# A hand-written order of 303 work steps, replaced by another order of the same steps

## The reference

```python
x = x + mixer_a(layernorm(x))       # projection to 5 k columns, causal conv over 4 taps, SiLU,
                                    # then attention with decay and Fenwick-level weights, 32 heads
x = x + ffn(layernorm(x))           # 16-head softmax attention, layernorm, 8 experts
                                    # (128 -> 256 -> 128) of which each token uses its best two
x = x + mixer_b(layernorm(x))       # value times 9 gates at 9 shifts along the sequence, layernorm
x = x + ffn(layernorm(x))           # the same ffn, same weights, a second time
```

## Time and profile before

| | us |
|---|---|
| median of 3 runs (2266.46 to 2270.33) | 2267.56 |
| the profiled execution | 2270.33 |
| its span, first to last instruction | 2268.5 |
| PE busy in the span | 2076.0 (92%) |
| DVE busy | 1775.4 (78%) |
| ACT busy | 1447.9 (64%) |
| POOL busy | 874.6 (39%) |

### The profile page before, as it was taken

One profiled execution on the slowest core, in us unless ns is written; L12 is line 12 of the kernel. 1 busy time (PEld: TensorE's weight loads), 2 busy tenths in 40 slices (PEclk: granted clock), 3 DMA queues, 4 the chain that ended last, 5 costly groups with the idle time before them and its releaser, 6 DMA issues. The chain is left out here.

```text
span 2268.5 us, 47559 instructions
## 1 busy us (share of the span) xinstructions
PE 2076.0 (92%) x16832; PEld 1620.4 (71%) x16832; DVE 1775.4 (78%) x4431; ACT 1447.9 (64%) x3113; POOL 874.6 (39%) x1204
## 2 busy tenths in 40 slices
PE   4879899999999999999999999999999999997766
...
PEclk9989999999999999999999999999999999998877
...
DMA packets 185820, 88.01 MB, mean 39 GB/s; under 512 B 118297, under 2 KB 179873, under 8 KB 180417
## 3 DMA queue, kind: packets, MB, share of 16 engines
...
...
## 5 line engine op out<-in xcount | busy, mean ns | idle before, releaser
L1261 DVE TENSOR_REDUCE nmax<-psB 128x2 f32<-128x512 f32 x512 | 315.6, 679 | 34.5 <-PE psB L741 34.4
L1186 DVE SCALAR_TENSOR_TENSOR work<-psA,c_conv_w,work 128x255 f32<-128x255 f32 (+2 forms) x810 | 330.0, 473 | 12.4 <-ACT work L926 12.2
L609 PE MATMUL psA<-xnT_a,c_w_in 128*128 128x256 f32 x1088 | 295.2, 399 | 31.8 <-DVE work L1186 22.7
L1009 ACT ACTIVATE pt<-psB 128x512 f32<-128x512 f32 x512 | 264.5, 609 | 46.1 <-PE psB L760 45.4
L845 PE MATMUL psB<-c_w,hid 128*128 128x128 f32 x2048 | 276.9, 281 | 2.6 <-DVE ff L1342 0.9
L845 PEld LDWEIGHTS psB<-c_w,hid 128*128 128x128 f32 x2048 | 259.9, 194 | 25.0 <-issue 10.1
L833 PE MATMUL psB<-x1T,c_w 128*128 128x256 f32 x1024 | 267.0, 391 | 0.9 <-DVE ff L1342 0.6
L1213 DVE TENSOR_TENSOR att<-att,QK 128x1024 f32<-128x1024 f32 x192 | 238.4, 1270 | 36.0 <-ACT att L963 34.2
L1494 POOL TENSOR_TENSOR own<-X,ccoef 128x512 f32<-128x512 f32 x128 | 160.9, 1266 | 258.5 <-PE psA L674 211.8
L1032 ACT ACTIVATE hid<-psB,c_b 128x256 f32<-128x256 f32 x496 | 211.2, 486 | 75.6 <-PE psB L833 72.3
L963 ACT ACTIVATE att<-psA 128x512 f32<-128x512 f32 x384 | 203.6, 611 | 69.7 <-PE psA L650 67.5
...
## 6 DMA issues: line engine op xcount, KB each, us to landing
qk_scr<-qparts SPq DMA_DIRECT2D x128, 192.0 KB, 3.6
...
low<-lvl_scr SPq DMA_DIRECT2D x256, 1.5 KB
...
```

The source lines that it names most:

```text
L609: e.matmul(t[:, 0:T], w_in[:, first + j * P:first + (j + 1) * P], xnT_a[:, :], start=True, stop=True).then_inc(filled[b], 1)
L1009: e.activation(pt_b[a % PTS][:, :, :].rearrange("p h q -> p (h q)"), t[:, :], ACT.Exp, scale=float(AD) ** -0.5).then_inc(drained[b], 1)
L1186: m = e.scalar_tensor_tensor(out=cv[:, back:], in0=t[:, 0:T - back], scalar=conv_w[:, c, tap:tap + 1], in1=cv[:, back:], op0=ALU.mult, op1 ...
L1261: e.tensor_reduce(nmax[:, i, 2 * h2:2 * h2 + 2], t[:, :].rearrange("p (h k) -> p h k", k=T), AX.X, ALU.max).then_inc(drained[b], 1)
```

## The change

The table `PERIOD` is replaced by another order of the same 303 hops. 292 hops keep their lag. Eleven have one less: `rowmax1.1`, `rowmax1.2`, `rowmax1.3`, `maxt1.0`, `v1.0`, `es1.0`, `exps1.0`, `outp0.2`, `gates0.6`, `place0.0` and `conv0.0`, and ten of them move from the head of a turn to the end of the turn before it, so that they come at nearly the same point of a sequence's life. `place0.0` moves from the middle of a turn to the end of the turn before it, 0.6 of a turn earlier for its sequence. The largest lag stays 5, the turns 21, the table loads of ACT 66. No instruction is added or taken away. L395 goes, and the wait of L603 is put on `conv0.0` and `zgate0.0` of sequence 0.

```diff
 PERIOD = """
-rowmax1.2+4 conv0.0+1 rowmax1.1+4 gates0.6+1 rowmax1.3+4 maxt1.0+4 outp0.2+2 v1.0+4 up0.0+3 fn0.0+2 relu0.0+3
...
+load_x0.0+0 tail0.5+3 up0.0+3 ep1.0+4 fn0.0+2 relu0.0+3 ocopy1.0+4 es1.1+4 lvl0.0+1 exps1.1+4 down1.6+5 fn0.1+2
...
-        first_w_in = next(hop for hop in hops if hop[0] in ("conv", "zgate"))
...
                 elif what in ("conv", "zgate"):
                     first = DIM + conv_tiles(k)[0] * P if what == "conv" else 2 * k * P
-                    if hop == first_w_in:
+                    if n == 0 and k == 0:
                         e.wait_ge(in_loaded, 16 * len(in_consts))
```

More of the change, by code:

```diff
@@ L109 @@
[L109 to L123, removed]
@@ L124 @@
-ep0.1+2 es0.2+2 prod0.3+1 sum0.1+1 ep0.2+2 q1.1+3 sum0.2+1 es0.3+2 sum0.3+1 gated0.1+1 ep0.3+2 exps0.3+2 gates0.3+0
-own0.4+1 gated0.0+1 gated0.2+1 ocopy0.3+2 gated0.3+1 weigh0.4+1 wexp0.4+1 gates0.4+0 wexp0.5+1 up1.5+4 prod0.4+1
-weigh0.5+1 tail0.0+2 sum0.4+1 relu1.5+4 relu1.6+4 own0.5+1 prod0.5+1 gated0.4+1 up1.6+4 wexp0.6+1 tail0.1+2 wexp0.7+1
-gates0.5+0 down1.5+4 weigh0.6+1 acc1.5+4 sum0.5+1 prod0.6+1 relu1.7+4 gated0.5+1 up1.7+4 own0.6+1 tail0.2+2 weigh0.7+1
-sum0.6+1 smax1.0+3 tail0.3+2 prod0.7+1 sum0.7+1 own0.7+1 tail0.4+2 smax1.2+3 outp0.0+1 smax1.1+3 ssq0.0+1 rowmax1.0+3
@@ L129 @@
-ssq0.1+1 ssq0.2+1 ssq0.3+1 smax1.3+3 gated0.6+1 outp0.1+1 gated0.7+1
+load_x0.0+0 tail0.5+3 up0.0+3 ep1.0+4 fn0.0+2 relu0.0+3 ocopy1.0+4 es1.1+4 lvl0.0+1 exps1.1+4 down1.6+5 fn0.1+2
+conv0.1+1 tail0.6+3 q0.0+2 experts0.0+3 ep1.1+4 acc1.6+5 tap0.0+1 ocopy1.1+4 experts0.1+3 es1.2+4 lvl0.1+1
+exps1.2+4 down1.7+5 q0.1+2 up0.1+3 conv0.2+1 taps0.0+1 acc1.7+5 ep1.2+4 down0.0+3 tap0.1+1 es1.3+4 relu0.1+3
+down0.1+3 tap0.2+1 taps0.1+1 acc0.0+3 up0.2+3 up0.3+3 ocopy1.2+4 acc0.1+3 exps1.3+4 relu0.2+3 down0.2+3
@@ new lines @@
+silu0.0+1 experts1.2+5 relu0.3+3 taps0.2+1 zgate0.0+1 acc0.2+3 up0.4+3 down0.3+3 zact0.0+1 conv0.3+1 up0.5+3
+relu0.4+3 tap0.3+1 down0.4+3 silu0.1+1 lvl0.2+1 xt0.0+1 silu0.2+1 conv0.4+1 gates0.0+0 relu0.5+3 acc0.3+3
+experts1.3+5 up0.6+3 up0.7+3 xt0.1+1 taps0.3+1 conv0.5+1 tap0.4+1 silu0.3+1 xcopy0.0+1 acc0.4+3 relu0.6+3
+down0.5+3 tap0.5+1 taps0.4+1 down0.6+3 xcopy0.1+1 relu0.7+3 zgate0.1+1 down0.7+3 xt0.2+1 taps0.5+1 zact0.1+1
+acc0.5+3 acc0.6+3 acc0.7+3 conv0.6+1 tap0.6+1 ep1.3+4 silu0.4+1 ocopy1.3+4 xcopy0.2+1 silu0.5+1 xt0.3+1
@@ new lines @@
+experts0.2+3 taps0.6+1 tail1.0+4 experts0.3+3 conv0.7+1 zgate0.2+1 tap0.7+1 bcp0.0+1 taps0.7+1 xcopy0.3+1
+zact0.2+1 tail1.1+4 mix1.0+3 v0.0+2 xt0.4+1 silu0.6+1 tail1.2+4 xcopy0.4+1 zgate0.3+1 tail1.3+4 silu0.7+1
+smax0.0+2 xt0.5+1 xt0.6+1 mix1.1+3 rowmax0.0+2 zact0.3+1 xcopy0.5+1 smax0.1+2 conv0.8+1 tap0.8+1 tail1.4+4
+smax0.2+2 lvl0.3+1 lvl0.4+1 lvl0.5+1 rowmax0.1+2 lvl0.6+1 xcopy0.6+1 rowmax0.2+2 mix1.2+3 mix1.3+3 tail1.5+4
+tail1.6+4 mix1.4+3 mix1.5+3 taps0.8+1 qk0.0+1 up1.0+4 up1.1+4 relu1.0+4 relu1.1+4 mix1.6+3 experts1.0+4 mix1.7+3
@@ new lines @@
+mix1.8+3 qkc0.0+1 coef0.0+1 experts1.1+4 zgate0.4+1 mix1.9+3 zact0.4+1 mix1.10+3 own0.0+1 down1.0+4 silu0.8+1
+zgate0.5+1 smax0.3+2 zgate0.6+1 zact0.5+1 acc1.0+4 rowmax0.3+2 mix1.11+3 zgate0.7+1 zact0.6+1 lvl0.7+1 up1.2+4
+relu1.2+4 zact0.7+1 maxt0.0+2 mix1.12+3 down1.1+4 acc1.1+4 up1.3+4 weigh0.0+1 weigh0.1+1 wexp0.0+1 down1.2+4
+weigh0.2+1 es0.0+2 prod0.0+1 relu1.3+4 sum0.0+1 wexp0.1+1 exps0.0+2 acc1.2+4 fn1.0+3 wexp0.2+1 down1.3+4
+own0.1+1 fn1.1+3 ep0.0+2 ocopy0.0+2 q1.0+3 gates0.1+0 prod0.1+1 xt0.7+1 es0.1+2 weigh0.3+1 own0.2+1 xcopy0.7+1
```

13 lines of the change are left out of this document (9 added, 4 removed).

## The result

The changed kernel takes 2329.9 us (median of 4 runs, 2328.3 to 2337.3) against 2267.6 for the kernel before (median of 3; a fourth execution of it, in the chip's slower state, took 2444.2 and is left out): the ratio is 1.027, 95% interval 1.025 to 1.030. It is 62 us slower; 31 were forecast (2299, against 2268). The direction was right, the size was half. The time lies inside the whole range given (2240 to 2340) and outside the forecast's own (2284 to 2318). The profiled execution has a span of 2333.7 us.

The account below looks back on a forecast made before the run. PE was taken as the bound, with waits for PSUM banks that DVE frees. New waits of 5.7 against 3.75 us, with 0.2 more, gave 2.2 a turn, 29 in 13 turns, plus 3 in filling: 2299 us, range 2240 to 2340.

Parts of the forecast that it names:

- filling: Turns 1 to 3, as the pipeline fills: the same DVE loops with less PE work between cost 3 us, bounds -5 and +15.
- the full turns: Turns 4 to 16, 13 of them: each about 2.2 us longer, 29 us together.
- place 2: Row maxima of layer 0 in the dense stretch: PE loses 1.3 us to DVE, and 0.4 at `zgate0.4`, a turn.
- The old waits go: Five PE waits for DVE in a full turn of the kernel before, 3.75 us together, all vanish.
- Place 1: `conv0.7` to `zgate0.3`: `xt0.4` waits 1.2 us a turn for the taps, and `conv0.7`'s own second bank costs 0.5.
- Place 3: End of the turn, `smax1.1` to `gates0.4`: PE waits for DVE and ACT, 2.1 us a turn, bounds 0.7 and 3.5.
- Elsewhere: `conv0.4`'s second bank costs 0.2 us a turn, `sum` and `weigh` banks behind `gated` steps 0.2; `place0.0` costs 0.
- The clock is left at 1.00: PE's clock in full turns: no new wait is much longer than 1.2 us, so it stays full.
- The rival: PE's clock falls to 0.93 in full turns: 8.8 us a turn, 115 in all, 2380 us; chance 0.03.
- Contention, 0 to +1 on DVE: DVE's `prod` and POOL's `own` are paired anew: 0 to +1 us of DVE a turn, taken as 0.
- The rival with DVE as the bound of the dense stretch: `acc0.5` to `taps0.8`: DVE has 27 us of work, PE 22; +5 us a turn, 2333 us; chance 0.16.
- The faster rival: DVE reaches `conv0.6` in step; only waits that hold with idle DVE remain, 1.9 us a turn: 2240 us; chance 0.24.

Follow-up runs that it names:

- xcopy_first: Changed kernel with `xcopy0.3` put ahead of `tap0.7`, which changes ACT's list alone: 2333.7 us, ratio 1.028 to the kernel before.
- outp_early: Changed kernel with `outp0.0` moved between `smax1.1` and `tail0.2`, and `maxt1.0` behind `outp0.1`: 2411.8 us, ratio 1.063 to the kernel before.
- fill_new: New table for turns 0 to 3, the old table from turn 4: 2287.3 us, ratio 1.0072 to the kernel before.
- place_back: Changed kernel with `place0.0` alone put back behind `xcopy0.6` in the middle of the turn, lag 1: 2346.4 us, ratio 1.034 to the kernel before.
- half_taps_before: Kernel before, with DVE's three taps of each convolution applied to the first 128 of 256 tokens only: 2257.2 us, ratio 0.995.
- half_taps_after: Changed kernel, with DVE's three taps of each convolution applied to the first 128 of 256 tokens only: 2286.6 us, ratio 1.007 to the kernel before.
- zgate_first: Changed kernel with `zgate0.2` put ahead of `conv0.7`, and `xcopy0.3` ahead of both: 2336.5 us, ratio 1.029 to the kernel before.
- smax3_later: Changed kernel with `smax0.3` one step later on PE, behind `zgate0.6`: 2331.0 us, ratio 1.027 to the kernel before.
- mended: Changed kernel with the moves of `zgate_first` and `smax3_later`, and `conv0.1` directly behind `es1.1`: 2332.6 us, ratio 1.029 to the kernel before.

## Why the prediction was right in direction and half in size

The mechanism, PE waiting for banks that DVE frees late, was right. Two terms of the sum were mis-sized: filling, put at 3 us, measured 18, and the full turns, put at 29, measured 43, with the largest part missed behind place 2, where the late DVE was taken as caught up.

- *The old waits go.* Right: I let go 3.75 us a turn, the table shows 4.9 gone. `gates0.4` stayed, and `v0.0`, `sum0.4` and `tail1.5`, which I had not priced, went too.
- *Place 1, 1.7.* It measured 2.28. The loop through the taps at `xt0.4` is there and is the bound, as `xcopy_first` shows: with ACT's wait gone the whole 1.88 stands at `xt0.4`. It was mis-sized by what DVE still had in front of it: its taps start some 0.8 us after ACT's.
- *Place 2, 1.7.* It measured 2.3 on the spot and 1.4 more behind it (`up1.1`, `smax0.3`). The sum ended at `zgate0.4` and took what came after as caught up; DVE was still late. This is the largest term missed in the full turns. The place holds the short falls of the clock too.
- *Place 3, 2.1.* It measured 1.0. `outp_early` shows that the new table's arrangement there is better than this one with `outp0.0` earlier.
- *Elsewhere, 0.4.* The head of the turn costs 1.0, where `down1.6` and `down1.7` directly follow `es1.1` and `es1.2` and want the banks that ACT is still emptying; I had not looked there. Put together: 8.0 new less 4.9 old, 3.1, against 3.28 measured by length and 2.2 forecast. 14 us of the 31 missing are here, 15 in filling and 2 in draining.
- *The clock is left at 1.00.* Wrong. It falls in 6 of 13 full turns, about 1.2 us each, 7 us in all, part of the 3.28. The rival had the mechanism with the wrong size: a short fall behind the dense stretch, not a whole turn at 0.93.
- *Filling, 3.* This step failed. It measured 18 (`fill_new`), outside the bounds of -5 and +15. I had taken half a full turn's loss for each turn, though PE's own rows there showed that these turns are made of waits. That `place0.0` makes nothing wait was wrong for turn 0: PE itself stands there for 4.1 us. Putting it back did not win that, so it isn't `place0.0` alone (`place_back`). Why the other hops lose is open. Shorter taps took 5 of the 20.6 us away (turn 4 starts at 339.0 and 323.7 in the pair of kernels with half taps).
- *Contention, 0 to +1 on DVE.* Wrong in sign: DVE's busy time is 4.0 us a turn less. A part of that is on PE's path. L1139 and L1141, which `gates0.4` waits for, take 2.1 us in turn 9 of the kernel before and 1.04 in the changed one. Place 3 had them at 1.2 by their size, not by the trace of before, and that this fitted was luck. What the rest is worth, no run separates.

The rival with DVE as the bound of the dense stretch gave 5 a turn and 2333. That the time came within 3 us of it is luck: its full turns were too dear (3.28) and it had no more for filling than the forecast. Its mechanism is borne out for about half of the distance (`half_taps_before` and `half_taps_after`). The faster rival's floor of 1.9 isn't the sum of its terms (0.9, 0.2, 0.9 and place 3's 0.7 are 2.7), so its 2240 was some 10 us too low by its own terms. That waits move rather than go when their cause stays (`xcopy_first`, `zgate_first`, `smax3_later`, `mended`) was in none of my cases. No order tried here beats the kernel before.
